# Three GIN layers and a graph attention block on one core: the last sum layer gathers rows as exact halves of 2 KB

## The chip, the cores and the metric

The kernel runs on one core of a Trainium2 chip. The time is that of one launch in device microseconds, of the slowest core (here the only one). Less is better.

## The reference

There are 6250 nodes of 256 channels and 100000 edges, sorted by destination. Layer norm and relu, then an attention block over the edges (8 heads, self loops added) with two batch norms and a feed-forward part, added to x. Then again layer norm and relu, and three sum layers:

```python
def gin(h, w, b, eps):
    agg = segment_sum(h[src], dst, num_segments=6250)
    return ((1 + eps) * h + agg) @ w + b
h = relu(gin(h, w1, b1, eps1))      # 256 -> 512
h = relu(gin(h, w2, b2, eps2))      # 512 -> 512
out = x + gin(h, w3, b3, eps3)      # 512 -> 256
```

The change is about the two last sum layers.

## The kernel before

The kernel works in stages, one after the other, with a barrier between them. Nodes come in 50 blocks of 125. A table in HBM holds the rows that edges read. The product with w3 is made before the last sum: the middle sum layer (`wide_layer`) already writes h @ w3, 256 channels, so the last layer only sums rows and adds the bias and x.

**The sum of a block** is made in one of two ways, in `mixed_layer` (first and last sum layer). Two of three blocks are dense: a part of an adjacency matrix of counts, stored earlier in HBM as bf16, is loaded in six parts of 250 or 281 KB (L1935), turned to float32r by ScalarE (L1942, three buffers), and TensorE multiplies 50 of its 125x125 pieces with rows that lie in SBUF (L2017, 512 columns: an upper half of few bits, and the exact rest). Every third block (1, 4, ..., 49) is gathered: GpSimd issues 17 indirect DMAs of 128 rows (L1828, each followed by a small memset that is waited for, L1832), VectorE makes 17 one-hot matrices, and TensorE multiplies them with the rows (L2036). The gather buffers are filled and emptied by quarters of 4, 4, 4 and 5 gathers: GpSimd waits on `quarters_used` before each quarter, TensorE on `rows_gathered`.

A dense block also runs at least one turn of a loop over edges that the matrix doesn't hold ("few" edges): SyncE loads 32 records (L1770), GpSimd gathers 32 rows (L1810), TensorE multiplies them (L2024) before it closes the block (L2044).

**The order on each engine** is written out by `over_steps` in six-block turns. GpSimd has, at step b, `gather_few(b)` and `gather(b + 2)`, so that around the gathered block g its order is: gather(g), few(g-1), few(g+1), gather(g+3), few(g+2), and so on. TensorE has the blocks in order; each begins with loads of its edge range from SBUF into registers (L1734), and the engine's own queue is in order, so that they stand behind any wait of the block before. SyncE loads few records, records, and, in the last layer, `load_own`: the block's own rows from the table and its rows of x1.

**The first sum layer** has `halves` set: rows of the table are 512 float32r values (2 KB: upper half and rest), there is one gather buffer (`GATHERS = 1`), and own rows come from SBUF (`rows_first`). **The last layer** has it not: the table's rows are 256 float32 values (1 KB), there are two gather buffers, one per gathered block in turn, float32 products take two passes, and own rows come by DMA. Its dense blocks use float32r halves all the same, from `rows_last` in SBUF.

**The middle layer** (`wide_layer`) gathers 2 KB rows for 46 of 50 blocks. It makes `rows_last`: ScalarE copies the product (`store`, L2351) and sends it to `table3` (L2353), VectorE cuts off the upper half and writes the rest to `rows_last` (`halve`, lag 4), and ScalarE copies the upper half there (`keep_upper`, L2357, lag 5). SyncE has `load_block`: records and own rows.

Of the kernel before, what the change touches and what calls it, by code (L numbers as in the profile page):

```python
# [6 lines left out]
F32 = mybir.dt.float32  # L7
# [90 lines left out]
def build(nc, x, src, dst, Wq, bq, Wk, bk, Wv, bv, Wo, bo, W1, b1, W2, b2, g1, be1, g2, be2,  # L98
# [2 lines left out]
    table0 = nc.dram_tensor("table0", (N, TW), F32).ap()  # L101
    table1 = nc.dram_tensor("table1", (N, 2 * D), F32R).ap()
    table2 = nc.dram_tensor("table2", (N, HID), F32).ap()
    table3 = nc.dram_tensor("table3", (N, D), F32).ap()
    x1 = nc.dram_tensor("x1", (N, D), F32).ap()
    pairs = nc.dram_tensor("pair_records", (E // ROW + ROWS, 2 * ROW), F32).ap()
    adjacency = nc.dram_tensor("adjacency", (BLOCKS, P, BLOCKS * NB), BF16).ap()
# [3 lines left out]
    with ExitStack() as ctx:  # L111
# [71 lines left out]
        def block_rows(table, b):  # L183
            return table[bass.ds(b * NB, NB), :]
# [1454 lines left out]

        def mixed_layer(n, table):  # L1640
            last_layer = n == 2
            halves = not last_layer
            row_width = 2 * D if halves else D
            kind = F32R if halves else F32
            k_tiles = D // P
            with ExitStack() as phase:
# [106 lines left out]
                @block.sync  # L1753
                def _(sp):
                    rounds, few = counters(sp, "sp_r"), counters(sp, "sp_f")

                    def load_weights():
                        if last_layer:
                            sp.dma_start(c3_sb[:, :], c3.partition_broadcast(NB)).then_inc(weights_loaded, 16)
                        else:  # L1760
                            for tile, w in ((w1_sb, w1), (w2_sb, w2)):
                                sp.dma_start(tile[:, :, :], w.rearrange("(k p) n -> p k n", p=P)).then_inc(weights_loaded, 16)

                    def load_few(k):
                        if not k.dense:
                            return
                        lo, hi = edge_range(sp, k)
                        with sp.Fori(lo, hi, OV) as at:
                            sp.wait_ge(few_used[k.t], few_of(sp, few[k.t]) + 1)
                            sp.dma_start(few_record[k.t][:, :], edges[bass.ds(at, OV), :]).then_inc(few_loaded[k.t], 16)  # L1770
                            sp.reg_add(few[k.t], few[k.t], 1)

                    def load_records(k):
                        if k.dense:
                            return
                        lo, hi = edge_range(sp, k)
                        with sp.Fori(lo, hi, RE) as at:

                            sp.wait_ge(round_gathered[k.t], count_of(sp, rounds[k.t]) + 1)
                            sp.dma_start(record[k.t][:, :, :].rearrange("p j c -> p (j c)"),  # L1780
                                         edges[bass.ds(at, RE), :].rearrange("(p j) c -> p (j c)", j=T)).then_inc(record_loaded[k.t], 16)
                            sp.reg_add(rounds[k.t], rounds[k.t], 1)

                    def load_own(k):
                        sp.wait_ge(own_used[k.s], k.i + 1)
                        sp.dma_start(own[k.s][:, :], block_rows(table, k.b)).then_inc(own_loaded[k.s], 16)
                        if last_layer:
                            sp.wait_ge(x1_used[k.s], k.i + 1)
                            sp.dma_start(x1_sb[k.s][:, :], block_rows(x1, k.b)).then_inc(x1_loaded[k.s], 16)

                    load_records(place(GATHERED_AT, 0))
                    if halves:
                        over_steps(sp, [(load_few, 0), (load_records, -2)], load_weights)
                    else:
                        over_steps(sp, [(load_few, 0), (load_records, -2), (load_own, 1)], load_weights)

                @block.gpsimd
                def _(pool):
# [41 lines left out]
                def _(dve):  # L1840
# [3 lines left out]
                    for s in range(2):  # L1844
                        dve.sem_inc(sums_read[s], 1)
                        if last_layer:
                            dve.sem_inc(own_used[s], 1)
                            dve.sem_inc(x1_used[s], 1)

                    def onehot_few(k):  # L1850
# [223 lines left out]
        def wide_layer(n, table, w):  # L2074
            k_tiles = w // P
            with ExitStack() as phase:
# [113 lines left out]
                def _(sp):  # L2190
# [21 lines left out]
                        sp.wait_ge(own_used[s], i + 1)  # L2212
                        sp.dma_start(own[s][:, :], block_rows(table, 2 * i + s)).then_inc(own_loaded[s], 16)

                    over_steps(sp, [(load_block, 0)])

                @block.gpsimd
                def _(pool):
# [117 lines left out]
                def _(act):  # L2336
                    for s in range(2):
                        act.sem_inc(result_ready[s], 1)
                        act.sem_inc(upper_ready[s], 1)
                        first_store(act, stored[s])  # L2340

                    def copy_turned(s, i):
                        act.wait_ge(sum_turned[s], i + 2)
# [3 lines left out]
                    def store(s, i):  # L2347
                        act.wait_ge(product[s], i + 1)
                        act.wait_ge(lower_ready[s], i + 1)
                        act.wait_ge(stored[s], (i + 1) * 16)  # L2350
                        act.activation(result[s][:, :], product_ps[0:NB, 0:D], ACT.Copy).then_inc(result_ready[s], 1)  # L2351
                        act.wait_ge(result_ready[s], i + 2)
                        act.dma_start(block_rows(table3, 2 * i + s), result[s][:, :]).then_inc(stored[s], 16)  # L2353

                    def keep_upper(s, i):
                        act.wait_ge(upper_cut[s], i + 1)
# [35 lines left out]
                        load_source(r, r)  # L2392
                    load_parts(0)
                    over_steps(act, [(load_weights, 0), (copy_turned, 1), (store, 2), (keep_upper, 5)], cast_source, AHEAD, AHEAD + 1)
                    for s in range(2):
                        act.wait_ge(stored[s], 16 * (PAIRS + 1))

                @block.tensor
                def _(pe):
# [106 lines left out]
```

## Time and profile before

| | us |
|---|---|
| median of 3 runs | 4893.87 (4884.36 to 4903.47) |
| the profiled execution | 4883.26 |
| its span, first to last instruction | 4881.6 |
| first sum layer in it | about 2312 to 3070 |
| middle sum layer | about 3070 to 4303 |
| last sum layer | about 4304 to 4882 |
| mean granted TensorE clock | 0.891 of full speed |

Engines: PE is TensorE's matmuls, PEld its weight loads, DVE VectorE, ACT ScalarE, POOL GpSimd, SP SyncE. A line of the timeline has the start, the time from the first start to the last end of the instructions merged in it, the engine, the source line, and in brackets how long the engine was idle before it and what ended that. Instructions that only handle registers or issue DMAs do not count as busy.

### The profile page before, as it was taken

The numbers are of one execution on the slowest core, as the hardware profiler recorded it, in microseconds if no ns is written. First come the engines' busy times: TensorE is split into PE (matmuls) and PEld (weight loads), VectorE is DVE, ScalarE is ACT, GpSimd is POOL, SyncE is SP. The second block draws the span as 40 slices with busy tenths as digits, with TensorE's granted clock in tenths as the row PEclk, the third lists the DMA queues.
The fourth block names the chain that finished last, engine by engine and source line by source line (L and its number), as shares of the span: only waits on it lengthen the run. The fifth ranks groups of instructions, "written<-read, shape, count | busy, mean of one in ns | idle before, by whom it ended". The sixth has DMA issues, their size and how long they took to land. (4 is left out here: it accounts for less than half of the span.)

```text
span 4881.6 us, 71170 instructions
## 1 busy us (share of the span) xinstructions
PE 3784.9 (78%) x15901; PEld 2477.0 (51%) x15902; DVE 2240.4 (46%) x7891; ACT 1436.5 (29%) x2745; POOL 2681.3 (55%) x4185
## 2 busy tenths in 40 slices
PE   3886645665566656885899999688888888879999
PEld 1233324444444444775677777344434444457777
DVE  6997756766677766345112111122222222323222
ACT  3983222222222222235344444100000000023333
POOL 6781056666667766013544444266666666656565
PEclk9999977777777777985999999899999999989999
DMA  4442133333333333016766667467777777656665
GB/s 138 172 183 98 58 81 94 96 96 94 95 94 97 95 96 90 0 55 168 212 193 200 179 184 204 133 200 209 212 209 210 210 217 207 192 158 207 201 202 179
DMA packets 346846, 734.87 MB, mean 151 GB/s; under 512 B 77407, under 2 KB 171229, under 8 KB 341985
## 3 DMA queue, kind: packets, MB, share of 16 engines
q0 software_dynamic: 176144, 461.72, 33.8%
q10 hardware_dynamic: 100178, 157.63, 10.2%
q1 hardware_dynamic: 70268, 113.00, 6.8%
q14 instruction: 204, 1.67, 0.1%
q8 instruction: 52, 0.85, 0.1%
HBM read 622.28 MB, written 109.84 MB: 150 GB/s over the span
## 5 line engine op out<-in xcount | busy, mean ns | idle before, releaser
L900 POOL DMA_INDIRECT a_gathered<-table,record x850 | 808.2, 951 | 642.4 <-issue 373.2
L2245 POOL DMA_INDIRECT l_gathered<-table,record x782 | 761.3, 974 | 470.4 <-issue 281.7
L2434 PE MATMUL bank<-l_gathered,l_onehot 128*125 128x512 f32 x1564 | 769.0, 645 | 191.0 <-DMA l_gathered<-table,record 92.0
L1828 POOL DMA_INDIRECT l_gathered<-table,record x578 | 545.6, 944 | 463.3 <-PE bank L2036 215.0
L1249 PE MATMUL bank<-a_gathered,a_onehot 128*125 128x264 f32 x1700 | 569.3, 493 | 105.1 <-DVE a_gathered L1053 90.9
L2434 PEld LDWEIGHTS bank<-l_gathered,l_onehot 128*125 128x125 f32 x1564 | 310.0, 203 | 627.2 <-issue 480.2
L1942 ACT ACTIVATE l_part<-l_packed 128x1000 fp32r<-128x1000 bf16 (+1 forms) x396 | 412.9, 1070 | 560.6 <-PE bank L2017 201.5
L1249 PEld LDWEIGHTS bank<-a_gathered,a_onehot 128*125 128x125 f32 x1700 | 393.1, 243 | 207.3 <-issue 66.5
L2017 PE MATMUL bank<-rows_first,l_part 125*125 125x512 f32 x1650 | 405.1, 405 | 30.3 <-ACT l_part L1942 30.3
L2017 PE MATMUL bank<-rows_last,l_part 125*125 125x512 f32 x1650 | 395.0, 398 | 11.5 <-ACT l_part L1942 11.5
L2017 PEld LDWEIGHTS bank<-rows_first,l_part 125*125 125x125 f32 x1650 | 307.8, 187 | 121.4 <-issue 43.9
L2017 PEld LDWEIGHTS bank<-rows_last,l_part 125*125 125x125 f32 x1650 | 304.5, 186 | 89.8 <-issue 10.3
L615 PE MATMUL bank<-d_code_hot,d_low_hot 128*128 128x250 bf16 x875 | 268.7, 386 | 51.7 <-DVE d_code_hot L570 24.4
L587 ACT ACTIVATE d_stage<-bank 128x500 bf16<-128x500 f32 (+1 forms) x432 | 287.6, 726 | 34.8 <-PE bank L615 27.2
L1053 DVE TENSOR_TENSOR a_gathered<-a_gathered,bank 128x1024 f32<-128x1024 f32 x200 | 244.0, 1283 | 41.8 <-ACT bank L1192 30.9
L2344 ACT ACTIVATE l_zT<-bank 128x500 f32<-128x500 f32 x50 | 29.3, 587 | 772.3 <-issue 460.0
L1892 DVE SCALAR_TENSOR_TENSOR l_work<-rows_first,one_eps,bank 125x256 f32<-125x256 f32 x50 | 24.0, 481 | 495.9 <-PE bank L2044 460.5
L570 DVE TENSOR_SCALAR d_code_hot<-d_code_iota,d_lists 128x250 bf16<-128x250 bf16 x875 | 246.9, 319 | 0.0
L2036 PE MATMUL bank<-l_gathered,l_onehot 128*125 128x256 f32 (+1 forms) x867 | 209.2, 398 | 18.3 <-DMA l_gathered<-table,record 18.3
L2304 DVE TENSOR_SCALAR l_source_cut<-l_source_rows 125x512 int32<-125x512 int32 x50 | 21.5, 430 | 435.8 <-remote 342.2
L615 PEld LDWEIGHTS bank<-d_code_hot,d_low_hot 128*128 128x128 bf16 x875 | 91.0, 104 | 228.6 <-DVE d_code_hot L570 79.4
L569 DVE TENSOR_SCALAR d_low_hot<-d_low_iota,d_lists 128x128 bf16<-128x128 bf16 x645 | 196.7, 307 | 1.2 <-ACT d_lists L577 1.2
(282 smaller groups left out, 5571.9 us busy)
## 6 DMA issues: line engine op xcount, KB each, us to landing
l_packed<-adjacency ACTq DMA_DIRECT2D x265, 250.0 KB
adjacency<-d_stage SPq DMA_DIRECT2D x35, 1562.5 KB
l_packed<-adjacency ACTq DMA_DIRECT2D x132, 281.2 KB
l_gathered<-table,record POOLq DMA_INDIRECT x1360
a_gathered<-table,record POOLq DMA_INDIRECT x850
table<-rows_first POOLq DMA_DIRECT2D x50, 250.0 KB, 3.6
table<-l_work ACTq DMA_DIRECT2D x50, 250.0 KB
l_source_rows<-table ACTq DMA_DIRECT2D x50, 250.0 KB
```

The lines of the kernel that those rows point to most:

```text
L570: dve.tensor_scalar(code_hot[g % HOT][:, :], code_iota[:, :], lists[:, c, 1, k:k + 1], None, ALU.is_equal).then_inc(pair_ready, 1)
L587: act.activation(*evict(d, h), ACT.Copy).then_inc(summed_read, 1)
L615: pe.matmul(banks[n % 7][:, (g - g0) * CODES:(g - g0 + 1) * CODES], low_hot[at % HOT][:, :], code_hot[at % HOT][:, :], start=True, stop=Tr ...
L900: pool.indirect_dma_start(out=gathered0[s][:, j * TW:(j + 1) * TW], out_offset=None, in_=table0, in_offset=bass.IndirectOffsetOnAxis(ap=re ...
L1053: dve.tensor_tensor(values[:, j0:j1], values[:, j0:j1], factors[:, j0:j1, :].unsqueeze(3).broadcast_to([P, j1 - j0, HEADS, DH]), ALU.mult) ...
L1249: last = pe.matmul(acc_ps[s][0:NB, 0:TW], onehot[s][:, j, :], rows[:, j, :], start=(j == 0), stop=(j == T - 1), skip_group_check=True)
L1828: pool.indirect_dma_start(out=gathered[g][:, j, :], out_offset=None, in_=table, in_offset=bass.IndirectOffsetOnAxis(ap=record[k.t][:, j, 0 ...
L1942: act.activation(part[r][:, 0:h1 - h0, :].rearrange("p h n -> p (h n)"), packed[r][:, 0:h1 - h0, :].rearrange("p h n -> p (h n)"), ACT.Cop ...
L2017: last = pe.matmul(sum_ps[k.s][0:NB, :], part[r][0:NB, h - h0, :], rows_sb[:, h, :], start=(h == 0), stop=False, skip_group_check=True)
L2036: last = pe.matmul(total, onehot[k.t][:, j, :], gathered[g][:, j, :], start=False, stop=(j == T - 1), skip_group_check=True)
L2245: pool.indirect_dma_start(out=gathered[:, j * w:(j + 1) * w], out_offset=None, in_=table, in_offset=bass.IndirectOffsetOnAxis(ap=record[t] ...
L2434: last = pe.matmul(total[0:NB, 0:w], onehot[t][:, j, :], rows[:, j, :], start=False, stop=(j == T - 1), skip_group_check=True)
```

## The change

The last layer gets `halves` as the first one has it. Its table has rows of 512 float32r values (upper half and rest, 2 KB). The gathered products are one float32r pass of 512 columns in place of two float32 passes of 256. There is one gather buffer of [128, 17, 512] in place of two of [128, 17, 256]. Own rows are read from `rows_last`, in two additions and a third that joins the halves, and their DMA goes.

In the middle layer ScalarE no longer stores to the table; SyncE stores the finished rows of `rows_last` (250 KB a block) as a second stage of its order, six steps behind its loads, and waits for both halves.

```diff
-    table3 = nc.dram_tensor("table3", (N, D), F32).ap()
+    table3 = nc.dram_tensor("table3", (N, 2 * D), F32R).ap()
...
-            halves = not last_layer
+            halves = True
...
-                    def load_own(k):
-                        sp.wait_ge(own_used[k.s], k.i + 1)
-                        sp.dma_start(own[k.s][:, :], block_rows(table, k.b)).then_inc(own_loaded[k.s], 16)
-                        if last_layer:
-                            sp.wait_ge(x1_used[k.s], k.i + 1)
-                            sp.dma_start(x1_sb[k.s][:, :], block_rows(x1, k.b)).then_inc(x1_loaded[k.s], 16)
+                    def load_x1(k):
+                        sp.wait_ge(x1_used[k.s], k.i + 1)
+                        sp.dma_start(x1_sb[k.s][:, :], block_rows(x1, k.b)).then_inc(x1_loaded[k.s], 16)
...
-                        over_steps(sp, [(load_few, 0), (load_records, -2), (load_own, 1)], load_weights)
+                        over_steps(sp, [(load_few, 0), (load_records, -2), (load_x1, 1)], load_weights)
...
-                    over_steps(sp, [(load_block, 0)])
+                    def store_rows(s, i):
+                        wait_apart(sp, lower_ready[s], i + 2, 2)
+                        wait_apart(sp, upper_ready[s], i + 2, 2)
+                        sp.dma_start(block_rows(table3, 2 * i + s).bitcast(F32),
+                                     rows_last[:, bass.ds(2 * i + s, 1), :].rearrange("p o c -> p (o c)").bitcast(F32)).then_inc(stored[s], 16)
+
+                    over_steps(sp, [(load_block, 0), (store_rows, 6)])
+                    for s in range(2):
+                        sp.wait_ge(stored[s], 16 * PAIRS)
...
-                        first_store(act, stored[s])
...
-                        act.wait_ge(stored[s], (i + 1) * 16)
                         act.activation(result[s][:, :], product_ps[0:NB, 0:D], ACT.Copy).then_inc(result_ready[s], 1)
-                        act.wait_ge(result_ready[s], i + 2)
-                        act.dma_start(block_rows(table3, 2 * i + s), result[s][:, :]).then_inc(stored[s], 16)
```

## Rows read from the trace of the kernel before

**Rows 1.** The page: its first line.
```profile
span 4881.6 us, 71170 instructions
```

**Rows 2.** Windows of the last layer: busy time by engine, granted clock, DMA share, GB/s.
```profile
4376.00:4730.00 354.00, 353.32 (x1531) 276.69 (x1530) 100.90 (x346) 133.66 (x128) 215.37 (x392) 1.00 0.67 202
```

**Rows 3.** Groups of the last layer by line and shape: busy, mean ns, idle before.
```profile
L2017 PE MATMUL bank<-rows_last,l_part 125*125 125x512 f32 x1650 | 395.0, 398 | 11.5 <-ACT l_part L1942 11.5
...
L1828 POOL DMA_INDIRECT l_gathered<-table,record x289 | 274.5, 950 | 139.1 <-issue 86.9 <-POOL stats L1832 52.2
...
L2036 PE MATMUL bank<-l_gathered,l_onehot 128*125 128x256 f32 x578 | 132.3, 388 | 7.2 <-DMA l_gathered<-table,record 7.2
```

**Rows 4.** Timeline of GpSimd in the last layer.
```profile
4374.23 0.95 POOL L1828 DMA_INDIRECT l_gathered<-table,record  x1 [1.46 <-issue]
...
4800.62 0.95 POOL L1828 DMA_INDIRECT l_gathered<-table,record  x1 [1.33 <-issue]
...
4825.31 0.96 POOL L1828 DMA_INDIRECT l_gathered<-table,record  x1 [0.27 <-POOL stats L1832]
4828.78 0.88 POOL L1810 DMA_INDIRECT l_few_rows<-table,l_few_record  x1 [2.40 <-issue]
...
4833.15 0.95 POOL L1828 DMA_INDIRECT l_gathered<-table,record  x1 [1.44 <-issue]
...
4860.43 0.88 POOL L1810 DMA_INDIRECT l_few_rows<-table,l_few_record  x1 [2.81 <-issue]
```

**Rows 5.** Timeline of TensorE in the last layer.
```profile
4803.29 7.50 PE L2036 MATMUL bank<-l_gathered,l_onehot 128*125 128x256 f32 x34
...
4835.85 7.50 PE L2036 MATMUL bank<-l_gathered,l_onehot 128*125 128x256 f32 x34
...
4875.75 0.17 PE L2044 MATMUL bank<-zeros 128*125 128x2 bf16 x1
```

**Rows 6.** Timeline of the last layer, two places where TensorE waits for few rows.
```profile
4369.81 0.88 POOL L1810 DMA_INDIRECT l_few_rows<-table,l_few_record  x1 [2.75 <-issue]
...
4372.20 1.21 PE L2024 MATMUL bank<-l_few_rows,l_few_onehot 32*125 32x256 f32 x2 [6.03 <-DMA l_few_rows<-table,l_few_record]
...
4374.06 4.20 PE L2036 MATMUL bank<-l_gathered,l_onehot 128*125 128x256 f32 x9
...
4730.39 0.98 POOL L1810 DMA_INDIRECT l_few_rows<-table,l_few_record  x1 [2.99 <-issue]
...
4735.95 0.69 PE L2024 MATMUL bank<-l_few_rows,l_few_onehot 32*125 32x256 f32 x2 [0.19 <-DMA l_few_rows<-table,l_few_record]
...
4738.06 7.60 PE L2036 MATMUL bank<-l_gathered,l_onehot 128*125 128x256 f32 x34
```

**Rows 7.** Timelines of GpSimd and TensorE in the first sum layer.
```profile
2375.29 0.87 POOL L1810 DMA_INDIRECT l_few_rows<-table,l_few_record  x1 [2.42 <-issue]
...
2387.27 0.94 POOL L1828 DMA_INDIRECT l_gathered<-table,record  x1 [9.05 <-PE bank L2036]
...
2335.17 2.07 PE L2036 MATMUL bank<-l_gathered,l_onehot 128*125 128x512 f32 x4 [3.86 <-DMA l_gathered<-table,record]
...
2379.18 0.49 PE L2024 MATMUL bank<-l_few_rows,l_few_onehot 32*125 32x512 f32 x1 [1.64 <-DMA l_few_rows<-table,l_few_record]
...
2385.18 4.30 PE L2036 MATMUL bank<-l_gathered,l_onehot 128*125 128x512 f32 x17
```

**Rows 8.** Windows of the first sum layer: columns as in the group of windows above.
```profile
2357.00:2365.00 8.00, 8.00 (x45) 6.40 (x44) 1.29 (x3) 3.92 (x5) 5.93 (x11) 1.00 1.00 284
```

**Rows 9.** Timelines of the middle layer, its end, and the page's list of DMA issues.
```profile
3779.04 0.95 POOL L2245 DMA_INDIRECT l_gathered<-table,record  x1 [3.62 <-PE bank L2434]
...
3782.14 0.36 SPq L2209 DMA_DIRECT2D record<-edge_records  x1
...
4304.42 0.56 ACTq L181 DMA_DIRECT2D spare<-identity  x2
...
table<-rows_first POOLq DMA_DIRECT2D x50, 250.0 KB, 3.6
```

More of the change, by code:

```diff
@@ L1782, in load_records @@
                             sp.reg_add(rounds[k.t], rounds[k.t], 1)
-                    def load_own(k):
-                        sp.wait_ge(own_used[k.s], k.i + 1)
-                        sp.dma_start(own[k.s][:, :], block_rows(table, k.b)).then_inc(own_loaded[k.s], 16)
-                        if last_layer:
-                            sp.wait_ge(x1_used[k.s], k.i + 1)
-                            sp.dma_start(x1_sb[k.s][:, :], block_rows(x1, k.b)).then_inc(x1_loaded[k.s], 16)
+                    def load_x1(k):
+                        sp.wait_ge(x1_used[k.s], k.i + 1)
+                        sp.dma_start(x1_sb[k.s][:, :], block_rows(x1, k.b)).then_inc(x1_loaded[k.s], 16)
                     load_records(place(GATHERED_AT, 0))
-                    if halves:
+                    if last_layer:
+                        over_steps(sp, [(load_few, 0), (load_records, -2), (load_x1, 1)], load_weights)
+                    else:
                         over_steps(sp, [(load_few, 0), (load_records, -2)], load_weights)
-                    else:
-                        over_steps(sp, [(load_few, 0), (load_records, -2), (load_own, 1)], load_weights)
                 @block.gpsimd
@@ L1846, in _ @@
                         if last_layer:
-                            dve.sem_inc(own_used[s], 1)
                             dve.sem_inc(x1_used[s], 1)
@@ L2394, in _ @@
                     over_steps(act, [(load_weights, 0), (copy_turned, 1), (store, 2), (keep_upper, 5)], cast_source, AHEAD, AHEAD + 1)
-                    for s in range(2):
-                        act.wait_ge(stored[s], 16 * (PAIRS + 1))
                 @block.tensor
```

## The prediction

> **What bounds the kernel now.** I read the page first for the frame: the span is 4881.6 us [rows 1], the execution took 4883.26, and the median of the three runs is 4893.87. I make the sum against the profiled execution and add it to the median, which lies 10.6 us above. Half a per cent, 24.5 us, is about what a measurement of this kernel can tell from no change.
>
> Then the windows of the last layer. From 4376 to 4730 TensorE is busy 353.3 of 354 us at the full clock, with the DMA engines at 0.67 [rows 2]. That reads like a layer that TensorE bounds, and the change takes TensorE work away. The groups say what: 578 float32 passes of 256 columns [rows 3], 34 of them in 7.5 us for each gathered block [rows 5]; the first layer does the same block in 17 float32r passes, 4.3 us [rows 7]. So 3.2 us of each turn of three blocks would go, 17 times 3.2, some 54 us, if TensorE alone set the pace.
>
> So the next view must say whether anything else has the same pace. TensorE's turn is 4803.29 to 4835.85, 32.56 us [rows 5]. GpSimd's turn, first gather to first gather, is 4800.62 to 4833.15, 32.53 us [rows 4]; over the fourteen turns from 4374.23 to 4833.15 it is 32.78 us on average [rows 4]. Does GpSimd wait for TensorE there? Its gathers have 139 us of idle time before them in the whole layer, and the releasers are "issue" and its own memset, never TensorE [rows 3]. There are two gather buffers, and the one it fills at 4833.15 was emptied when TensorE's group of 4803.29 ended, 22 us earlier [rows 4, 5]. So GpSimd works at its own pace, and that is as slow as TensorE's. Its turn is made of the round of 17 gathers, 4800.62 to 4826.27 (25.65 us here; the seventeen rounds of the layer span 24.1 to 25.7, mean 24.5), and 8.3 us between rounds: 3.35 us on average until few(g-1) is issued (2.51 here), and 4.9 us more, in which few(g+1) is issued too, until the next round [rows 4]. None of that is in the diff. A gather costs GpSimd the same time whether its rows are 1 or 2 KB: 0.94 us in the first layer, 0.95 here [rows 4, 7].
>
> **The change part by part.**
>
> *TensorE's passes.* 3.2 us less a turn, and one pass of 0.2 us less for the few rows. At GpSimd's pace this is hidden: TensorE would then wait. It counts only once, at the layer's end.
>
> *One buffer in place of two.* This is the part that I take to decide. The next round, gather(g+3), may start only when TensorE has eaten the first quarter of block g. TensorE comes to block g only after few(g-1). GpSimd issues few(g-1) only after the whole round g. So a loop closes through both engines and a DMA: round g, few(g-1), its landing, TensorE's way to block g, four passes, and back to GpSimd. Before, the second buffer cut this loop.
>
> The terms, from the end of round g:
> - Until few(g-1) is issued: 3.35 us as before; 2.5 in the first layer, where SyncE has no own rows to load, as it has none after the change [rows 7]. I take 2.9.
> - Landing, from the start of the issuing instruction to TensorE's use of it, where TensorE stood waiting: 4369.81 to 4372.20, 2.4 us; 4730.39 to 4735.95, 5.6 us [rows 6]; in the first layer, with rows of 2 KB, 2375.29 to 2379.18, 3.9 us [rows 7]. I take 3.9, the nearest case and the middle one.
> - From the few product to the first gathered product, when TensorE had to wait: its queue is in order, so the loads of the next block's edge range stand behind the wait and now are exposed. 4372.20 to 4374.06 and 4735.95 to 4738.06, 1.9 and 2.1 us with two few passes [rows 6]; one of them goes, so 1.9.
> - From there to GpSimd's next gather: 2385.18 to 2387.27, 2.1 us at the full clock [rows 7].
> - The clock: after 3.9 us of idle time four passes took 2.07 us, 0.5 each, which is the 1.2 GHz level, where 17 in 4.30 us, 0.25 each, are the 2.4 GHz one [rows 7]; after 6.0 us idle nine float32 passes took 4.20 us, 0.47 each [rows 6], against 0.22 [rows 5]. TensorE's work in a turn would be 32.56 less 3.4, 29.2 us, so in a turn of 35 us or more it idles some 6 us, and I expect the first quarter at the low level: 1.0 us more. I take half of it, 0.5, since late parts may split the idle time.
>
> Sum: 2.9 + 3.9 + 1.9 + 2.1 + 0.5 = 11.3 us between rounds, against 8.3: 3.0 us a turn. Fourteen turns from the round of 4374.23 to that of 4833.15: **+42 us**.
>
> Two rules of the Trainium skill bear on this. The page "Trainium Kernel Development and Optimization", section Best Practices, says to double-buffer so that transfers overlap with computing; it speaks against this change. The page "TensorE: Matmul & The Clock Gate", section "Loop structure matters more than you think", says that a DMA wait between bursts of matmuls leaves the next burst at the slow clock; [rows 6, 7] agree. By the clock rule alone the first quarter would be wholly at the low level in every turn, 1.0 us in place of 0.5, which is 7 us more in all.
>
> *The first turns.* The buffers are free for the first two rounds. Round three starts at 4374.23 now [rows 4]; with few(3) issued at 4369.81 [rows 6] it would start at 4369.81 + 3.9 + 1.9 + 2.1 + 0.5 = 4378.2: **+4**.
>
> *The layer's end.* From the last few gather to TensorE's last product it is 4860.43 to 4875.92, 15.5 us, because TensorE is a dense block behind [rows 4, 5]. After, TensorE waits there: 3.9 + 1.9 + 4.3 + 0.2, and 1 for the clock, 11.3: **-4**. VectorE's finish has one more product and one more sum before the last store, by the 0.4 to 0.5 us that such an instruction of 256 columns takes: **+1**.
>
> *Loads of own rows go.* 125 KB of DMA a block, hidden before. Their waits in SyncE's queue go too; nothing waited for them. Nothing, apart from the 2.9 above.
>
> *More bytes.* A round moves 4.5 MB in place of 2.2. In the first layer the DMA engines are full, share 1.00 at 284 GB/s, while a round of 2 KB rows and matrix parts overlap [rows 8]. The last layer wants its parts faster. TensorE has some 5 us of slack a turn to absorb late parts; a few gather queued behind such a round may land late. That is the upper end: 5.6 us for the landing.
>
> *The middle layer.* The store moves to SyncE, which now waits for both halves of block b-6 before it loads the records of block b+1. Both halves are there when ScalarE has come through its step, which follows TensorE's step: some 4 to 10 us after the point of 3782.14, where SyncE now issues the next record load [rows 9]. GpSimd starts a round at 3779.04 and needs those records only at the next, 25 us later [rows 9]. A load issued up to 10 us late still comes some 8 us early: nothing; without that cover each late us would cost 46 us over 46 rounds. ScalarE's issue and wait go, off the path. The doubled store adds 125 KB to a turn that gathers 4.5 MB. But the last store now begins only after the last halves, right before the barrier, and is waited for: the 250 KB store at the earlier stage lands in 3.6 us [rows 9], and the next stage, whose first DMA is at 4304.42 [rows 9], starts that much later: **+4**, between 2 and 5.
>
> Sum: 42 + 4 - 4 + 1 + 4 = **+47 us**. For the profiled execution that is 4930; at the median, 4941.
>
> **The rivals.**
>
> *A, the forecast:* the loop through one buffer, 4941; its own range 4918 to 4965. Chance 0.55.
>
> *B, the few rows land fast* (2.4 us [rows 6]), and TensorE keeps its clock: 2.9 + 2.4 + 1.9 + 2.1 = 9.3, 1.0 a turn, 14 us; first turns +2, end -7, the rest +5: +14, 4908. For it: GpSimd leaves the DMA ring 3 us to drain before it issues few(g-1). Against it: the one case with 2 KB rows shows 3.9. Chance 0.22.
>
> *C, the transfers are what is short:* share 1.00 [rows 8]; landing 5.6 and the low clock: 3.35 + 5.6 + 1.9 + 3.1 = 14.0, 5.7 a turn, 80 us; first turns +6, end -3, rest +5: +88, 4982. If late parts hold TensorE up longer than its slack, it comes out here too. Chance 0.16.
>
> *D, the other side:* TensorE is the true bound, and GpSimd's gap between rounds only looks like its own, held by records or few records that come at TensorE's pace. The turn then falls toward 29.2, at most 3.4 us, and already at 1.8 us a turn the kernel would be faster by over 0.5%. With 3.0 a turn: -42, end -6, rest +5, 4851. For it: two paces that agree within 0.03 us [rows 4, 5] look like a coupling. Against it: no releaser of TensorE, and in the first layer, where TensorE is far slower, the same gap to the few gather is still 2.5 us [rows 7]. Chance 0.07.
>
> **How the numbers follow.** The range leaves out D and the far end of C: from 4900, somewhat under B, to 4982, C. Slower by over 0.5% means above 4918: A and C, less A's low edge, 0.70. Within: B, with that edge and part of D, 0.24. Faster: D, 0.06.
>
> **What would show it.** Right: GpSimd's first gather of a round is released by TensorE's L2036, 10 to 13 us after the last gather of the round before; TensorE is idle 4 to 7 us before the few product ahead of each gathered block, and is no longer at 99% busy; the turn is 35 to 36.5 us; the granted clock of the layer falls below 1. Wrong: no wait of GpSimd for L2036 (D), a gap near 9 (B), or waits of TensorE for parts inside dense blocks (C). In the middle layer turns stay at 25 us and its end moves by some 4. The prediction is wrong if few rows land under 3 us in most turns.

## The result, and the profile after

The changed kernel takes 5021.14 us (median of 4 runs, 5004.83 to 5023.53) against 4895.72 us: ratio 1.0272, 95% interval 1.025 to 1.0294. It is slower by 125 us, where 47 were forecast, and lies above the range. The profiled executions differ by more, 139.4 us between their spans; all rows of this section come from them.

The page, first line:

```profile
span 5021.0 us, 70683 instructions
```

The time is lost in two stages of nearly equal share. I cut both executions at the first gather of each layer. The first sum layer is equal (781.2 us before, 780.2 after). From the middle layer's first round to the last layer's first round 1213.0 us became 1284.3 (+71). From there to the end 568.2 became 630.4 (+62). The remaining 6 us lie ahead of the middle layer. The forecast had 4 for the middle layer and 43 for the last.

**The last layer.** Windows, columns as in [rows 2], then groups by line and shape:

```profile
4453.00:4900.00 447.00, 381.91 (x1476) 285.98 (x1476) 133.85 (x445) 149.48 (x144) 237.68 (x432) 0.91 0.80 231
```

```profile
L2013 PE MATMUL bank<-rows_last,l_part 125*125 125x512 f32 x1644 | 400.2, 402 | 13.2 <-issue 8.1 <-ACT l_part L1938 4.9
...
L1825 POOL DMA_INDIRECT l_gathered<-table,record x289 | 272.3, 942 | 209.6 <-PE bank L2032 97.6 <-POOL stats L1829 61.1 <-issue 50.9
...
L2032 PE MATMUL bank<-l_gathered,l_onehot 128*125 128x512 f32 x289 | 103.5, 529 | 10.6 <-DMA l_gathered<-table,record 10.6
...
L2020 PE MATMUL bank<-l_few_rows,l_few_onehot 32*125 32x512 f32 x33 | 19.2, 583 | 58.2 <-DMA l_few_rows<-table,l_few_record 58.2
```

TensorE is busy 85% of the stretch where it had 99.8 [rows 2], and the granted clock is 0.91. The gathered products take 103.5 us in place of 132.3 [rows 3]: the saved 29 us are real, and go into waiting. GpSimd's gathers now have 97.6 us of idle time that TensorE's products end, where there were none [rows 3]; TensorE itself waits 58.2 us for few rows. One turn shows both, GpSimd first, then TensorE:

```profile
4605.18 0.94 POOL L1825 DMA_INDIRECT l_gathered<-table,record  x1 [7.34 <-PE bank L2032]
...
4630.01 0.94 POOL L1825 DMA_INDIRECT l_gathered<-table,record  x1 [0.27 <-POOL stats L1829]
4634.05 0.87 POOL L1807 DMA_INDIRECT l_few_rows<-table,l_few_record  x1 [2.99 <-issue]
4636.30 0.86 POOL L1807 DMA_INDIRECT l_few_rows<-table,l_few_record  x1 [1.38 <-issue]
4642.11 0.95 POOL L1825 DMA_INDIRECT l_gathered<-table,record  x1 [4.95 <-PE bank L2032]
```

```profile
4620.84 11.89 PE L2013 MATMUL bank<-rows_last,l_part 125*125 125x512 f32 x50
4637.15 0.49 PE L2020 MATMUL bank<-l_few_rows,l_few_onehot 32*125 32x512 f32 x1 [4.41 <-DMA l_few_rows<-table,l_few_record]
4637.57 0.22 PE L2040 MATMUL bank<-zeros 128*125 128x2 bf16 x1
4638.91 0.68 PE L2024 MATMUL bank<-zeros 128*125 128x512 bf16 x1 [1.12 <-issue]
4639.26 6.61 PE L2032 MATMUL bank<-l_gathered,l_onehot 128*125 128x512 f32 x17
```

The few rows issued at 4634.05 are used at 4637.15; the first gathered product comes 2.1 us later; GpSimd may go on at 4642.11, 2.85 us after that. That is the loop of the forecast, each arm of it visible. Over the fourteen turns from the third round of the layer to its last, a turn is 37.12 us on average where it was 32.78. A round is 24.4 us as before; between rounds there are 12.7 us where there were 8.3.

**The middle layer.** What SyncE waits for, from the layer's first round to the next stage:

```profile
SPq L77 <- ACT rows_last L2357: 364.1, 30, 27.7
SPq L1646 <- PEq L1646: 79.2, 1, 79.2
SPq L2209 <- DVEq L2325: 28.7, 4, 22.2
SPq L2205 <- PE bank L2432: 26.0, 2, 19.0
SPq L2219 <- DMA table<-rows_last: 8.1, 1, 8.1
```

The first line is the wait for the upper half (364 us in 30 waits), in the helper at L77; the wait of the record load at L2205 for a free tile was the stage's main one before, and is nearly gone (26 us, where it was 380). So SyncE comes to the record load late. SyncE and GpSimd in the steady part:

```profile
3764.70 0.72 SPq L2214 DMA_DIRECT2D table<-rows_last  x1
3776.65 0.35 SPq L2205 DMA_DIRECT2D record<-edge_records  x1
...
3789.47 0.69 SPq L2214 DMA_DIRECT2D table<-rows_last  x1
3803.49 0.34 SPq L2205 DMA_DIRECT2D record<-edge_records  x1
```

```profile
3752.67 1.00 POOL L2249 DMA_INDIRECT l_gathered<-table,record  x1 [8.10 <-issue]
...
3779.49 0.94 POOL L2249 DMA_INDIRECT l_gathered<-table,record  x1 [5.68 <-PE bank L2432]
...
3806.27 0.95 POOL L2249 DMA_INDIRECT l_gathered<-table,record  x1 [5.63 <-PE bank L2432]
```

Before, the record load came 3.1 us after the start of GpSimd's round in the turn that was read [rows 9]. That was nearly the earliest: over the 36 steady turns in which the changed kernel has a store ahead of the load, it came 3.1 to 9.5 us after, 5.6 on average. Here it is 21.9 us on average, and 24.0 in the two turns shown (3752.67 to 3776.65, 3779.49 to 3803.49); there GpSimd starts 2.8 us after the load. The bracket names TensorE, whose buffer was another condition; that both intervals from the load are 2.8 us, as at the layer's end below, says that the records came last. 24.0 + 2.8 is the turn of 26.8. Of the 36 turns 16 are longer than 25.5 us, and nine of these start 2.7 to 2.9 us after their load; the other seven, 1.9 to 5.0 us after it, are not explained one by one. With the undisturbed ones the turns from the third to the last but three are 25.74 us on average against 24.99, some 30 us over the layer.

At the end of the layer it is worse. There every second block has its full edges summed from a matrix and gathers few rows only, the order is written out without a loop, and SyncE does this:

```profile
4284.39 0.28 SPq L2214 DMA_DIRECT2D table<-rows_last  x1
4287.25 0.36 SPq L2205 DMA_DIRECT2D record<-edge_records  x1
...
4322.99 0.28 SPq L2214 DMA_DIRECT2D table<-rows_last  x1
4325.88 0.36 SPq L2205 DMA_DIRECT2D record<-edge_records  x1
...
4360.58 11.30 SPq L2214 DMA_DIRECT2D table<-rows_last  x7
```

and GpSimd:

```profile
4290.04 0.95 POOL L2249 DMA_INDIRECT l_gathered<-table,record  x1 [14.80 <-issue]
...
4328.68 0.95 POOL L2249 DMA_INDIRECT l_gathered<-table,record  x1 [16.28 <-issue]
```

Each round starts 2.8 us after its records were asked for, with 15 to 16 us of idle time before it. The round, TensorE's products of it, the halves (of an older block, but ScalarE comes to them only after those products), the store, the record load and the next round now stand in one chain. The last three turns are 37.7, 37.6 and 38.6 us where they were 26.3, 26.4 and 28.3: 33 us for three turns. From the last round's end to the next stage's first DMA it is 31.7 us in place of 23.2, with seven stores left to SyncE at 4360.58 and 8.1 us of waiting for the last.

### The profile page after: what moved, and what is told of

It is laid out like the page before. It is cut to its first block and busy times, and to the rows that moved or that the text cites. A ratio compares the mean times of both kernels' runs of the same rounds, so it can differ in the third digit from the quotient of the medians.

```text
span 5021.0 us, 70683 instructions
## 1 busy us (share of the span) xinstructions
PE 3788.4 (75%) x15579; PEld 2459.3 (49%) x15580; DVE 2262.0 (45%) x7958; ACT 1429.0 (28%) x2745; POOL 2678.8 (53%) x4185
## 5 line engine op out<-in xcount | busy, mean ns | idle before, releaser
L2432 PE MATMUL bank<-l_gathered,l_onehot 128*125 128x512 f32 x1564 | 785.0, 659 | 238.1 <-DMA l_gathered<-table,record 127.3
L2432 PEld LDWEIGHTS bank<-l_gathered,l_onehot 128*125 128x125 f32 x1564 | 320.4, 210 | 680.5 <-issue 512.3
L2013 PE MATMUL bank<-rows_last,l_part 125*125 125x512 f32 x1650 | 402.9, 403 | 31.7 <-ACT l_part L1938 23.4
L2013 PEld LDWEIGHTS bank<-rows_first,l_part 125*125 125x125 f32 x1650 | 307.9, 187 | 122.6 <-issue 46.5
L2032 PE MATMUL bank<-l_gathered,l_onehot 128*125 128x512 f32 x578 | 179.5, 472 | 21.2 <-DMA l_gathered<-table,record 21.2
L1264 PE MATMUL bank<-identity_bf,a_onehot_bf 128*128 128x128 bf16 x850 | 82.3, 235 | 147.3 <-ACT a_onehotT L1175 87.1
```

Of the source, the lines that this page charges most:

```text
L2013: last = pe.matmul(sum_ps[k.s][0:NB, :], part[r][0:NB, h - h0, :], rows_sb[:, h, :], start=(h == 0), stop=False, skip_group_check=True)
L2032: last = pe.matmul(total, onehot[k.t][:, j, :], gathered[g][:, j, :], start=False, stop=(j == T - 1), skip_group_check=True)
L2432: last = pe.matmul(total[0:NB, 0:w], onehot[t][:, j, :], rows[:, j, :], start=False, stop=(j == T - 1), skip_group_check=True)
```

## The experiments

The runs fell on several chips, and the kernel before differs between them by up to 6%. So each kernel is judged by its ratio on its own chip, and stages only against a trace from a chip on which the kernel before takes the same time. The kernels of the first table ran on two chips on which that is 4695.46 and 4693.96 us; there the middle layer's turns are 21.6 us, not 25.0. I call these two the second kind of chip.

| kernel | us | ratio, 95% interval | middle layer | last layer | turn, between rounds |
|---|---|---|---|---|---|
| before | 4695.36 | | 1066.2 | 574.0 | 33.1, 8.5 |
| changed | 4862.12 | 1.0356 (1.0338 to 1.0373) | 1174.0 | 628.7 | 37.1, 12.7 |
| changed, ScalarE stores | 4762.71 | 1.0154 (1.0137 to 1.0171) | 1074.5 | 627.9 | 36.9, 12.5 |
| changed, store 8 steps behind | 4765.06 | 1.0149 (1.0132 to 1.0166) | 1075.6 | 628.1 | 37.2, 12.8 |
| before, one gather buffer | 4766.35 | 1.0152 (1.0135 to 1.0169) | 1066.5 | 642.3 | 37.9, 13.3 |
| before, SyncE stores halves too | 4866.58 | 1.037 (1.0352 to 1.0387) | 1229.3 | 574.1 | 33.3, 8.7 |
| changed, few rows first | 4801.0 | 1.0225 (1.0208 to 1.0242) | 1179.3 | 562.8 | 33.1, 8.6 |
| changed, ScalarE stores, few rows first | 4699.56 | 1.0007 (0.9998 to 1.0017) | 1079.3 | 562.2 | 33.0, 8.4 |

The columns of layers are first gather to first gather, and first gather to end, in the profiled executions. The turns are those of the last layer.

**The kernel before and the changed kernel again.** No edit.

> The kernel before, unchanged, to have its stages on the chip of these runs. No theory is at stake: the last layer at 565 to 577 us; the middle layer either at turns of 25.0 us, as in the first profile, or at 21.5, as the experiments so far had it.

> The changed kernel, unchanged, beside the kernel before on the same chip. Both theories together (SyncE's order in the middle layer, the loop in the last): the last layer about 60 us longer than before wherever it runs. If the middle layer of the kernel before has turns of 21.5 us, SyncE's path has less to hide behind and costs 105 us there rather than 77: ratio about 1.035. If only the first chip's numbers hold, 1.027.

The loss repeats: 108 us in the middle layer, 55 in the last. The last three turns of the middle layer lose 37 us and its end 5.5, much as on the first chip; the steady turns lose 66 where they lost 30, 23.24 us on average against 21.60. They lose it in another way. SyncE and GpSimd in one of them:

```profile
3503.42 0.29 SPq L2214 DMA_DIRECT2D table<-rows_last  x1
3506.38 0.36 SPq L2205 DMA_DIRECT2D record<-edge_records  x1
```

```profile
3515.84 1.00 POOL L2249 DMA_INDIRECT l_gathered<-table,record  x1 [2.69 <-DMA record<-edge_records]
```

The record load follows the store by 3.0 us, not 12, and goes out 14.3 us after the start of GpSimd's round (3492.10); over the 36 turns with a store ahead of it that is 13.8 us on average, where the kernel before on this kind of chip has 8.1. It is only some 6 us late. But GpSimd has no idle time here to hide it in (0.30 us between rounds in the kernel before), and in 29 of the 36 turns GpSimd starts late, 8.2 to 12.0 us after the load, not 2.8. These loads go out while a round is being gathered; why they take so long was not tested here.

**ScalarE issues the store of the halves, SyncE has its old order.**

```diff
-                    over_steps(sp, [(load_block, 0), (store_rows, 6)])
+                    over_steps(sp, [(load_block, 0)])
...
-                    over_steps(act, [(load_weights, 0), (copy_turned, 1), (store, 2), (keep_upper, 5)], cast_source, AHEAD, AHEAD + 1)
+                    over_steps(act, [(load_weights, 0), (copy_turned, 1), (store, 2), (keep_upper, 5), (store_rows, 6)], cast_source, AHEAD, AHEAD + 1)
```

> The changed kernel with the store of the finished rows issued by ScalarE (a stage six steps behind), so that SyncE has only loads again; bytes, rows and the last layer stay. Theory one (the record loads stand behind the store in SyncE's order): the middle layer falls from 1276 us, first round to the next stage, back to about 1206, the total by some 70 us to about 4950. Rival (the doubled bytes of the store slow the gathers): the middle layer stays near 1270 and the total near 5020. Under both the last layer keeps turns of 37 us.

The 250 KB stores stay, the middle layer is back to 1074.5. So it is SyncE's queue, not the doubled bytes.

**SyncE stores, eight steps behind its loads in place of six.**

```diff
-                    over_steps(sp, [(load_block, 0), (store_rows, 6)])
+                    over_steps(sp, [(load_block, 0), (store_rows, 8)], head=10, tail=8)
```

> The changed kernel with SyncE's store eight steps behind its loads in place of six, so that both halves have long been there and SyncE does not wait for them. If the wait for the halves is what holds the record loads up, the middle layer comes back to that of the kernel before, within 15 us. If it is the time that SyncE's own register instructions take behind a store of 250 KB (0.7 us each in the changed kernel's trace), part of the loss stays: over 30 us.

SyncE still issues each store ahead of the next record load, but the halves are there when it comes to it. The waits of SyncE in the middle layer, of the changed kernel and then of this one:

```profile
SPq L77 <- ACT rows_last L2357: 809.3, 44, 27.0
SPq L2205 <- PE bank L2432: 113.3, 5, 52.5
```

```profile
SPq L2205 <- PE bank L2432: 680.9, 41, 51.6
...
SPq L77 <- ACT rows_last L2357: 25.2, 4, 18.0
```

The two waits have changed places and the layer is back to 1075.6. On this kind of chip, then, the wait is the cause, not the issuing; the first chip's long way from the store to the load is met below, in the last kernel with both mends. Nine us over the layer of before remain in both kernels; they lie behind the last round (stores that are left and waited for).

**The kernel before with one gather buffer in the last layer.** Rows of 1 KB, float32 products.

```diff
-                GATHERS = 1 if halves else 2
+                GATHERS = 1
...
-                    return 0 if halves else k.t
+                    return 0
```

> The kernel before with one gather buffer in the last layer in place of two; rows stay 1 KB of float32. Theory two (the loop through one buffer costs it): about 12.5 us between rounds in place of 8.3, turns of 36 to 37 us, the last layer 55 us longer, total about 4950. Rival (rows of 2 KB are what is short, one buffer alone is cheap): the few rows land in 2.4 us, the gap stays under 9.5, total under 4912.

This edit alone loses more in the last layer (68 us) than the whole change does there (55), and more than the 55 expected. The 2 KB rows are not needed for the loss. They are not free either: the few rows land after 3.9 us on average here (14 turns, 3.1 to 5.3), and after 4.7 in the changed kernel with ScalarE's store on the same chip. What makes this kernel's gap the longer one, 13.3 us, is the first quarter, 4.2 us from the first gathered product to GpSimd's next gather where the one-pass products need 2.85. A turn with usual values, GpSimd and TensorE:

```profile
4292.47 0.88 POOL L1810 DMA_INDIRECT l_few_rows<-table,l_few_record  x1 [3.00 <-issue]
4302.86 0.95 POOL L1828 DMA_INDIRECT l_gathered<-table,record  x1 [6.39 <-PE bank L2036]
```

```profile
4296.56 0.69 PE L2024 MATMUL bank<-l_few_rows,l_few_onehot 32*125 32x256 f32 x2 [2.04 <-DMA l_few_rows<-table,l_few_record]
```

So the shorter products give back 1.3 us a turn, and the 2 KB rows take some 0.8 of it again. The rule of the Trainium skill that the forecast named, double-buffering ("Trainium Kernel Development and Optimization", section Best Practices), is borne out here with its price.

**The kernel before, to which SyncE's store of the halves is added**, into a tensor that nothing reads; ScalarE's own store stays.

```diff
+                    over_steps(sp, [(load_block, 0), (store_rows, 6)])
-                    over_steps(sp, [(load_block, 0)])
```

> The kernel before, with one thing added: SyncE also stores the finished halves, 250 KB a block, to a table that nobody reads, six steps behind its loads. Theory one (SyncE's order): it costs all that the changed kernel lost in the middle layer, 70 to 77 us, total 4965 to 4975, and the last layer is untouched at 577 us. Rival (ScalarE's missing store or the changed last layer play a part): clearly less than 70.

The last layer is untouched (574.1), the middle layer loses 163 us, more than the change does (108) and more than the 70 to 77 expected. SyncE's store alone is enough for the loss. 109 us of it lie in the steady turns and 46 in the last three; why the pair of stores costs more than the one was not taken apart.

**The changed kernel, few rows first.** In the last layer SyncE loads and GpSimd gathers few(g-1) ahead of round g, not behind it.

```diff
-                        over_steps(sp, [(load_few, 0), (load_records, -2), (load_x1, 1)], load_weights)
+                        load_few(place(0, 0))
+                        over_steps(sp, [(load_few, -1), (load_records, -2), (load_x1, 1)], load_weights)
...
-                    over_steps(pool, [(gather_few, 0), (gather, -2)], lambda: gather(place(GATHERED_AT, 0)))
+                        gather_few(place(0, 0))
+                        over_steps(pool, [(gather_few, -1), (gather, -2)], lambda: gather(place(GATHERED_AT, 0)))
```

> The changed kernel, with the few rows of block g-1 loaded and gathered ahead of the round of block g in the last layer (SyncE's and GpSimd's order alone). Theory two (the few rows close the loop): TensorE no longer waits 3 to 6 us for few rows, the gap between rounds falls from 12.7 to GpSimd's own 7.5 to 8.5, turns to 32 to 33 us, total about 4950 with the middle layer unchanged at 1276. Rival (the transfers are saturated): TensorE waits for the last quarter or for matrix parts instead, turns stay over 35 us, total over 4990.

One buffer stays, and the loss is gone: the gap between rounds falls by 4.1 us, the layer by 66 us, to 11 us under the kernel before. TensorE now comes to block g at about the end of round g (in most rounds between 1.1 us before it and 0.8 us after, where it was 10 us after), and GpSimd's waits for TensorE's products are 2.3 us in the layer, where they were 97.6 in the first profile. So it is the loop through few(g-1), not the single buffer as such.

**Both mends together.** ScalarE stores, few rows first.

> The changed kernel with both mends: ScalarE issues the store of the finished rows, and the few rows of block g-1 are gathered ahead of the round of block g in the last layer. If both theories hold and the parts add up, the middle layer is that of the kernel before and the last layer is about 563 us, as with the second mend alone: within 0.5% of the kernel before, perhaps 5 to 15 us faster. If a third loss is hidden in the change, it stays over 1.01.

The two losses account for the whole, within 0.2%. But the saved TensorE work brings next to nothing: a turn of the last layer is 33.0 us, a round of 24.5 and 8.4 between rounds, as before. The layer is 12 us shorter by its start and its end, and the end of the middle layer takes 13 back. The two largest waits of GpSimd in that last layer are on its own memset and on its own instructions:

```profile
POOL l_gathered L1826 <- POOL stats L1830: 104.6, 270, 0.9
...
POOL l_few_rows L1808 <- issue: 55.9, 24, 3.5
```

**Both mends in another form**, the store by SyncE eight steps behind and few rows first, on a chip like the first one (before 4891.66, middle turns 25.0).

> The changed kernel with both mends in another form: SyncE keeps the store of the halves but issues it eight steps behind its loads in place of six, and in the last layer the few rows of block g-1 are gathered before round g. If the two losses are the wait in SyncE's queue and the loop through one buffer, and nothing else, it comes out as the kernel with ScalarE's store and few rows first did: ratio to before 0.998 to 1.004, on whichever chip. Rival: part of the middle layer's loss depends on the chip's pace there (turns of 25.0 or of 21.6 us), and the ratio is 1.005 or more on a chip with the long turns.

4890.98 us, ratio 0.9995 (0.998 to 1.001). The middle layer is 1226.2 us, the last 566.6. The account holds on both kinds of chip. It also says which half of the first chip's lateness costs: SyncE still issues the store ahead of the record load, and its way from one to the other can still be slow (below), but with the halves ready it begins early enough. The load goes out 3.0 to 10.6 us after the start of the round, 6.2 on average, nearly as before, and the steady turns are back at 25.0.

**Without the memset behind each gather.** Three kernels on a chip on which before takes 4972.88 us: the kernel before with few rows first; the changed kernel with both mends and no memset in the last layer; the kernel before with few rows first and no memset.

```diff
-                                    paused.step(pool.memset(pause, 0.0))
+                                    if not last_layer:
+                                        paused.step(pool.memset(pause, 0.0))
```

> The kernel before, whose two gather buffers and 1 KB rows stay; only GpSimd's order in the last layer changes: the few rows of block g-1 are gathered before the round of block g, not behind it. If TensorE and GpSimd both have a pace of 32.5 us a turn in the last layer and TensorE waits for almost nothing there, the turn stays between 32.6 and 33.2 us and the time within 0.3% of before. Rival: the few rows that TensorE waits for here and there (two to six us each) are worth something even before, and the last layer ends 5 to 10 us earlier (ratio 0.998).

> The changed kernel with both mends (ScalarE stores the halves in the middle layer; few rows of block g-1 gathered before round g), and in the last layer no memset behind each gather. Theory: what keeps the kernel with both mends from being faster than before is GpSimd's own pace, 24.4 us for a round of 17 gathers and 8.4 us between rounds. A gather takes 0.95 us and 1.4 us pass from gather to gather, so without the memset and the wait for it a round falls to 17 to 20 us and the turn to what TensorE needs, 29 to 30.5 us: the last layer 562 to some 520, ratio 0.990 to 0.993. Rival: the transfers of 2 KB rows and of matrix parts are what is short (DMA share 0.89 in the layer with both mends); then the round gets shorter, the idle time moves to waits for rows and parts, and the turn stays within 0.5 us of 33.0, ratio 0.999 to 1.003.

> The kernel before with the same two edits of GpSimd's order in the last layer (few rows first, no memset behind a gather), and nothing of the change. Theory: with 1 KB rows TensorE is the bound as soon as GpSimd is not, at 32.5 us a turn; so the turn stays at 32.5 to 32.8 and the time within 0.2% of before, and any gain of the kernel with both mends and no memset is a gain of the change's shorter TensorE work. Rival: GpSimd alone was the bound before and TensorE only filled its pace; then this kernel gains as much as the other, 1.5 us a turn or more, ratio 0.993 or less.

| kernel | us | ratio, 95% interval | last layer | turn | round, between rounds |
|---|---|---|---|---|---|
| before, few rows first | 4962.53 | 0.9986 (0.9964 to 1.0009) | 581.7 | 34.4 | 24.6, 9.8 |
| both mends, no memset | 5127.9 | 1.0312 (1.0278 to 1.0347) | 718.8 | 43.0 | 21.0, 22.0 |
| before, few rows first, no memset | 5162.0 | 1.0388 (1.0362 to 1.0414) | 781.4 | 46.5 | 21.1, 25.4 |

The first is no change that can be told. The other two miss both of their theories: the round gets 3.5 us shorter as expected, and the pause behind it 12 to 16 us longer. In the layer with both mends and no memset, GpSimd, then the issuing queues of SyncE and ScalarE with ScalarE's work:

```profile
4612.20 1.10 POOL L1808 DMA_INDIRECT l_few_rows<-table,l_few_record  x1 [10.99 <-DMA l_few_record<-edge_records]
4616.05 0.94 POOL L1826 DMA_INDIRECT l_gathered<-table,record  x1 [2.75 <-issue]
...
4635.95 0.94 POOL L1826 DMA_INDIRECT l_gathered<-table,record  x1 [0.30 <-issue]
4642.86 0.86 POOL L1808 DMA_INDIRECT l_few_rows<-table,l_few_record  x1 [5.97 <-DMA l_few_record<-edge_records]
```

```profile
4620.61 1.36 ACTq L1937 DMA_DIRECT2D l_packed<-adjacency  x3
4625.49 1.14 ACT L1944 ACTIVATE l_part<-l_packed 128x1125 fp32r<-128x1125 bf16 x1 [4.09 <-DMA l_packed<-adjacency]
4640.23 1.14 ACT L1944 ACTIVATE l_part<-l_packed 128x1125 fp32r<-128x1125 bf16 x1 [13.60 <-DMA found<-in_dst,cut_row_int]
4640.54 0.34 ACTq L1937 DMA_DIRECT2D l_packed<-adjacency  x1
```

Three matrix parts are asked for at 4620.61, inside the round. The first is used at 4625.49, 4.9 us later. The second is not used before 4640.23, 3.3 us after the round's last gather has ended (the name in the bracket is the profile's guess; L1944 reads `l_packed`). It is a pattern: in 13 of the 17 rounds ScalarE gets a part 3.3 to 3.5 us after the round's end. With the memsets it has a part some 4 to 6 us after asking. The few record comes late in the same way. So the memsets are not idle time to be saved: with them the other queues' transfers land during the round. By what means a memset does that is not shown.

## Why the prediction was wrong, point by point

**The step that failed** is "The middle layer", and in it "A load issued up to 10 us late still comes some 8 us early: nothing". Two things were wrong. The lateness: the halves of block b-6 came 12.0 us after the start of GpSimd's round (3752.67 to 3764.70), 9 us later than the record load of before in the turn of [rows 9], as foreseen; but the record load stood another 12.0 us behind the store (3764.70 to 3776.65), and I had given the way from one to the other nothing. Together 21 us late, and the slack is 25 less 2.8 and 3.1, some 19. (The 3.1 was an early case; by the average of 5.6 the load is 18 us late with 17 of slack, the same outcome.) And the end of the layer: I took the turns as all alike, where the last three have one record load in two steps, and ahead of it a wait for halves that ScalarE makes only after TensorE's products of the very block gathered in the round before (these end at 4281.35, the store goes out at 4284.39, the load at 4287.25); 33 us. The store at the end cost 8.5 us where 4 were forecast, since seven stores are left, not one. Sum: 30 + 33 + 8.5, against the 71 measured. That both are the wait in SyncE's order is shown: the store eight steps behind, and the store by ScalarE, each give all but 9 us back on the second kind of chip, and the former with few rows first all but 13 us on the first. The prediction had said what it costs "without that cover": 46 us for each late us. It was the right warning, given no chance among the rivals.

**The loop through one buffer** was right as a mechanism, in every arm, and its size was short: 37.12 less 32.78, times 14, is 61 us against +42. (The first turns gave +5 against +4 and the end -3 against -3, which makes the 62.) The terms of the gap, forecast and measured over the turns of the last layer: until few(g-1) is issued 2.9 and 2.9; landing 3.9 and about 5.0 (3.1 to 5.5); few product to first gathered product 1.9 and 2.1; from there to GpSimd's gather, clock included, 2.6 and 2.85 in most turns. The mis-sized one is the landing, 1.1 us over the forecast. With 1 KB rows it is 3.9 us on average (the kernel before with one buffer), so the size of the rows, or what else differs between these two kernels, is worth 0.8 to 1.0 us of it; what holds the transfers up is not shown. The low clock for the first quarter is the other short term: 2.85 us in twelve of fourteen turns, 1.98 and 2.42 in the other two, of which the first came after only 0.5 us of idle time, so nearly the whole microsecond was due and not half of it. Seventeen passes took 6.6 us at 4639.26 where they take 4.3 at the full clock [rows 7]. By the rule of the Trainium skill ("TensorE: Matmul & The Clock Gate", section "Loop structure matters more than you think") it would have been so in every turn, and the trace nearly agrees.

**TensorE's passes**: 3.2 us less a turn, hidden, right; even with the loop opened the turn is 33.0 us.

**The layer's end**: forecast 11.3 us from the last few gather to TensorE's last product; measured 5002.90 to 5014.59, 11.7.

**GpSimd at its own pace**, right: with TensorE's work 3 us a turn shorter and no loop, nothing is gained. What the forecast did not say, and the last experiments show, is that part of this pace is a pause that the other queues need.

**The rivals.** B (few rows land fast) and D (TensorE the true bound) did not occur. The last layer lies midway between A and C: 12.7 us between rounds against 11.3 and 14.0, a loss of 62 us against 43 and 84. Of C's terms the low clock came, and half of the longer landing. Its reason, transfers running short, is not shown; that the landing is shorter with 1 KB rows speaks for it. The total of 125 us is above C because of the middle layer, for which no rival stood.

## What to carry to other kernels

A store put into an in-order queue ahead of loads makes every later load wait for what the store waits for: work out, from the profile, when its data are ready and when the next load was issued, in each kind of turn and at the unrolled end, before calling it hidden. A single buffer was harmless here once nothing that its consumer needs was issued behind the producer's whole round; moving that one small transfer ahead was worth as much as the second buffer. And work taken from an engine that another one keeps pace with brings nothing until the other one's pace has been explained.

## What was not expected of the hardware

Seventeen gathers issued 1.25 us apart, with no memset between them, hold up direct DMAs of the other queues: parts that land some 4 to 6 us after issue with a memset and its wait in between (1.3 us a gather in most cases, up to 1.9 in others) land up to 20 us after issue without, after the round's end. The middle layer's gathers have no memset in any of these kernels, and its late record loads on the second kind of chip (8 to 12 us, above) look like the same thing. The DMA queues in the window 4615 to 4637 of the kernel with both mends and no memset (packets, MB, share of 16 engines; q0 carries GpSimd's indirect gathers, q10 ScalarE's parts):

```profile
q0 software_dynamic: 2209, 4.02, 68.9%
q10 hardware_dynamic: 560, 0.96, 13.2%
q1 hardware_dynamic: 242, 0.24, 3.3%
```

The shares go roughly with the bytes that each queue moved, and they leave 15% of the engines' time unused, so they don't explain a part that waits. The Trainium skill, "DMA: Bandwidth & Descriptors", section Queues, rings and completion order, says that each engine goes round between the queues that have work, one packet at a time; by that alone the parts should not have to wait for the end of the round. Whether they wait in the engines or before them these runs do not show.

On the first chip the way from SyncE's store to its next record load was 5.5 to 16 us in the steady part, 11 on average (3764.70 to 3776.65), with no wait in it that the trace shows, and 2.9 us at the layer's end; in the changed kernel on the second kind of chip it was 2.1 to 4.0 us in the steady part too. The way holds the same instructions on registers in both; at 3764.70 most of them take 0.7 us each, on the other chip most take under 0.2. The middle layer's turn is 25.0 to 25.2 us in the executions on some chips and 21.6 on the two of the first table, with the first sum layer equal. Neither was followed up.
